# Four small pieces of the opening stage moved to other places in the order of VectorE and ScalarE

## What is computed

```python
xn = _layernorm(x, axis=-1)
x = x + _L0_attn_ref(xn, ...) + _L0_ffn_ref(xn, ...)

# attention: 2 sequences of 1024 tokens, width 256, 16 heads of 16
qkv = xn @ qkv_w.T + qkv_b
scores = q @ k.T / 4 + slopes[h] * (pos_k - pos_q), causal
out = softmax(scores) @ v @ out_w.T + out_b

# experts: 16 of width 128, two for each token
scores = sigmoid(xn @ gate_w)
_, selected = top_k(scores + expert_bias, 2)
routed = sum over the two of weight * (silu(g) * u @ experts_down[e])
shared = silu(xn @ shared_gate_w) * (xn @ shared_up_w) @ shared_down_w
```

## Time and profile before

| | us |
|---|---|
| median of 3 runs | 494.85 (493.16 to 495.5) |
| profiled execution | 498.53 |
| its span in the trace | 496.7 |

### The profile page before, as it was taken

How to read it: one execution, slowest core, us unless ns; L and a number is a source line. 1 busy time by engine, 2 the same in 40 slices (tenths; PEclk the granted TensorE clock), 3 DMA queues, 4 the chain that set the end, 5 groups by cost and what they waited for, 6 DMA issues and landing times.

```text
span 496.7 us, 8349 instructions
## 1 busy us (share of the span) xinstructions
PE 435.9 (88%) x2973; PEld 256.1 (52%) x2973; DVE 324.2 (65%) x602; ACT 248.6 (50%) x567; POOL 181.3 (37%) x200
## 2 busy tenths in 40 slices
PE   3588963489699999998999999999999999999896
PEld 3447842267477667774444344444444444434444
DVE  2869761184457566678875867758687676872366
ACT  1632240130233334334766767667676676766650
POOL 2290677412700000001888887876110100920000
PEclk9799995599999999999999999999999999999999
DMA  8887994168989995434218339173160300002122
GB/s 260 171 355 270 368 326 169 63 214 258 199 181 240 221 247 155 128 96 137 62 46 158 74 73 160 45 130 45 35 114 2 78 18 3 1 2 50 39 69 84
DMA packets 50489, 66.41 MB, mean 134 GB/s; under 512 B 12433, under 2 KB 43285, under 8 KB 48883
## 3 DMA queue, kind: packets, MB, share of 16 engines
q1 hardware_dynamic: 45667, 55.18, 42.1%
q0 software_dynamic: 3680, 10.31, 8.3%
q10 hardware_dynamic: 1104, 0.41, 0.3%
HBM read 39.30 MB, written 27.25 MB: 134 GB/s over the span
## 4 chain that ended last, share of the span: by engine, by line
PE 63%; DVE 15%; DMA 7%; ACT 5%; another core or an unknown queue 5%; issue 4%; SPq 1%; DVEq 0%; ACTq 0%
PE ps L1330 14%; PE ps L1314 11%; PE ps L1302 11%; PE ps L1225 7%; DVE mx L1055 6%; DMA x_in<-sorted_tokens 5%; PE ps L1241 4%; PE ps L1317 3%; PE ps L1303 2%; PE ps L1352 2%; PE ps L1216 2%; DMA x_sb<-x 2%; PE ps L1172 2%; ACT pt L778 2%
## 5 line engine op out<-in xcount | busy, mean ns | idle before, releaser
L778 ACT ACTIVATE pt<-ps 128x512 f32<-128x512 f32 (+3 forms) x384 | 166.7, 492 | 75.3 <-PE ps L1317 48.5
L1055 DVE TENSOR_REDUCE mx<-ps 128x1 f32<-128x384 f32 (+6 forms) x189 | 153.8, 863 | 48.7 <-PE ps L1303 47.3
L1330 PE MATMUL ps<-pt,vg 128*32 128x512 f32 (+3 forms) x768 | 71.9, 492 | 0.0
L619 POOL DMA_INDIRECT yg<-sorted_outputs,slot_i x32 | 32.3, 1011 | 104.4 <-DMA sorted_outputs<-y_out 96.0
L1314 PE MATMUL ps<-qk 111*128 111x512 bf16 (+3 forms) x192 | 54.6, 328 | 3.1 <-ACT pt L778 1.6
L1314 PE MATMUL ps<-qs,ks 111*128 111x512 bf16 (+3 forms) x192 | 55.1, 327 | 0.8
L1225 PE MATMUL ps<-w_gu,hx 128*128 x192 | 52.1, 395 | 3.3 <-issue 1.6
L1302 PE MATMUL ps<-qk 108*128 108x512 bf16 (+3 forms) x192 | 50.2, 328 | 2.7 <-DVE mx L1055 2.2
L1317 PE MATMUL ps<-cbf 128*128 128x128 bf16 x256 | 52.2, 220 | 0.0
L1303 PE MATMUL ps<-cbf 128*128 128x128 bf16 x224 | 46.4, 220 | 0.0
L751 ACT ACTIVATE hx<-ps 128x384 f32<-128x384 f32 (+1 forms) x48 | 22.9, 478 | 40.0 <-PE ps L1216 38.3
(11 more groups left out here) (177 smaller groups left out, 695.1 us busy)
## 6 DMA issues: line engine op xcount, KB each, us to landing
sorted_tokens<-y_out SPq DMA_DIRECT2D x12, 512.0 KB, 5.0
qk_parts<-parts SPq DMA_DIRECT2D x16, 384.0 KB
x_in<-sorted_tokens SPq DMA_DIRECT2D x48, 128.0 KB, 4.9
sorted_outputs<-y_out SPq DMA_DIRECT2D x48, 128.0 KB, 3.0
qk<-qk_parts SPq DMA_DIRECT2D x8, 384.0 KB
w_gu<-e_gu SPq DMA_DIRECT2D x1, 2816.0 KB
x_sb<-x SPq DMA_DIRECT2D x4, 512.0 KB, 9.4
w_dn<-e_dn SPq DMA_DIRECT2D x1, 2048.0 KB
```

Of the source, the lines that this page charges most:

```text
L619: g_.indirect_dma_start(out=yg[:, n % 4, :], out_offset=None, in_=ysd, in_offset=bass.IndirectOffsetOnAxis(ap=slot_i[:, k, t:t + 1], axis= ...
L778: sc.activation(pt[:, s % 4, j, lo:CH], bank(n % 3)[:, lo:CH], ACT.Exp).then_inc(s_exp, 1)
L1055: last = v.reduce_max(dst, src, axis=AX.X)
L1330: ins = te.matmul(ps[32 * j:32 * j + 32, OUT_BANK * CH + lo:(OUT_BANK + 1) * CH], vg[:, par, kb, j, :], pt[:, s % 4, j, lo:CH], start=kb = ...
```

## The change

On ScalarE the high parts of the first two token jobs (numbers 6 and 7) are written between root 2 and root 3, in place of after wsh. On VectorE two weight low parts (jobs 0 and 1) are written after normalise 0 and ahead of statistics 2; and normalise 2, which makes quarter 2's shift, stands ahead of statistics 3 in place of behind it. The other four wl stay where they were. Nothing else differs; the number of instructions on each engine is the same.

```diff
@@ ScalarE
                 if q == 0:
                     for n in range(X0):
                         high(n)
+                if q == 2:
+                    for n in range(X0, X0 + 2):
+                        high(n)
             for q in (2, 3):
                 act.wait_ge(s_shift, q - 1)
...
-            for n in range(X0, G0):
-                high(n)
-            for n in range(G0, NJ):
+            for n in range(X0 + 2, NJ):
                 high(n)
@@ VectorE
-            for q in range(4):
+            for q in range(2):
                 statistics(q)
-                if q in (1, 2):
-                    normalise(q - 1)
-            for q in (2, 3):
-                normalise(q)
-            for n in range(X0):
+            normalise(0)
+            for n in range(2):
+                low(n)
+            statistics(2)
+            normalise(1)
+            normalise(2)
+            statistics(3)
+            normalise(3)
+            for n in range(2, X0):
                 low(n)
```

## The result

| | before | changed |
|---|---|---|
| median, 9 runs each | 494.27 us | 497.73 us |
| ratio of the runs | | 1.0062, 95% interval 1.0037 to 1.0087 |
| profiled execution | 498.53 us | 499.29 us |
| its span | 496.7 us | 497.5 us |
| median, 12 more runs of the changed kernel, 35 of before | 495.34 us | 497.72 us |

A forecast was written before the change was run, and what follows sets the result against it. It took the chain of waits up to the logits to bound this part, with VectorE late until 18.46 us and ScalarE after. Median 494.85 plus 0.92 (order) and 1.1 (clock) gave 496.9 us, range 494.2 to 499.3.

The forecast's parts named there:

- The order on VectorE: Ahead of statistics 3: two wl (0.66 us) and the shift (0.26) delay root 3, first xn and logits by 0.92 us.
- The hole of ScalarE and the early banks: Two xh between root 2 and root 3, and TensorE's earlier transposes of tiles 4 to 7, are hidden: 0 us.
- The clock: Logits: thinner TensorE work ahead leaves some 6 products at 1.2 GHz, 0.19 us more each, 1.1 us.
- Handing on: From slot_i through the 32 scatters to later stages: the delay of some 2 us moves with the path.
- the rival of absorption: Between 78.40 and 97.51 us: a standstill ended by weight loads swallows the delay, 494.85 us; chance 0.06.
- The sum: Whole kernel: 0.92 us of shift and 1.1 us of clock make 2.0 us, median 496.9 us; chance 0.40.
- clock late: Logit stage: 11 products at 1.2 GHz cost 2.1 us, 497.9 us; chance 0.22 together with one more wait.
- Faster by luck further on: Wait of 7.02 us for a tile's load at 160.51 goes if transfers collide less: 489.9 us; chance 0.07.

The follow-up runs named there:

- four wl: The kernel before with four wl in place of two ahead of statistics 2 on VectorE, nothing else: 498.37 us, ratio 1.0041.
- its parts alone: Two kernels, each the kernel before plus one part: two wl ahead of statistics 2, 496.71 us; normalise 2 ahead of statistics 3, 496.00 us.
- VectorE's part: The changed kernel with the two xh back behind wsh on ScalarE, VectorE's new order kept: 497.12 us, ratio 1.0040.
- one-row kernel: The changed kernel, but TensorE's job 8 waits for ScalarE's first xn, so the 24 transposes are one row: 495.14 us, again 496.11 us.
- the kernel with 3.8 us of delay: The kernel before with four unused additions on VectorE right ahead of the choice of experts: 500.32 us, ratio 1.0097.
- shift alone: The kernel before with normalise 2 ahead of statistics 3 and nothing else: 496.00 us, ratio 1.0028.
- two xh alone: The kernel before with two xh between root 2 and root 3 on ScalarE, VectorE as before: 495.45 us, ratio 1.0028.
- small weights in the hole: The kernel before with gwh, wsh and two xh between root 2 and root 3 on ScalarE: 494.09 us, ratio 0.9983.
- o between the g jobs: The kernel with gwh, wsh and two xh in ScalarE's hole, plus the two o jobs between the second and third g job: 494.42 us, ratio 0.9974.

## Why the prediction was right, and where not

**The order on VectorE** (0.92 us): right. 0.89 us at the first xn, 0.91 at the logits; 0.66 and 0.23 us for its parts alone, 1.33 for four wl. Costs by the pitch between neighbours were right, costs by the full duration (1.17) would not have been.

**The hole of ScalarE and the early banks** (0): right. The two xh change nothing on the path, no table load appeared, VectorE's idle time took up what was saved ahead of gwl.

**The clock** (1.1 us): the size was right, by luck as far as the reason goes. The extra time of the logits was 1.5, 1.0 and 1.1 us in the profiles of the change and of VectorE's part of it. My reason was that the split transposes bring the clock back late. But one row of transposes, which by this reason had to cure it, left 9.07 and 8.98 us; and in five of seven profiles the clock was back ahead of the logits and fell again at their start or inside them, a course that I had in no case. Only the other two went as forecast, with a clock that came back inside the logits.

**Handing on**: right against the rival of absorption, by the kernel with 3.8 us of delay. The end of the standstill moves with the scatters. The one-row kernel, late at slot_i by 1.8 us and by its runs hardly slower than before, stays unexplained.

**The sum**: 2.0 us forecast, 1.9 at slot_i in the first profile (1.4 to 1.5 in the second and in VectorE's part; each some 0.4 more against the profiles of shift alone and two xh alone, with their short first addition), and 3.5 and 2.4 us on the medians of two sets of runs. 497.73 lies inside the range, at the place of the case "clock late" (497.9), and by the first set beyond the 0.5% which I had called no difference with a chance of 0.58. (The range's upper end is 499.2 by its own sum, not 499.3.) Of the term behind slot_i, where I had 0, the runs decide nothing: by the medians up to 1.5 us are left over, but 2.0 us, a ratio of 1.0041, lies in the intervals of both sets. How many q/k parts get through before the scatters end is a candidate that I had not seen.

**Faster by luck further on**: a misreading. The wait of 7.02 us at 160.51 isn't in the chain of the changed kernel, and nothing was gained: from the first expert tokens on TensorE to the attention it took 102.2 us before and 102.6 after. A wait in the chain of an iterating stage names one of several things that end nearly together, and isn't a price.

## What to carry to other kernels

An instruction that is put into another place pays with its pitch on the engine that is late there, and gains only where its old place was on the path; look for the idle time behind its old place first. Here the late engine was loaded (two wl, a shift) so that an engine with spare time could be ahead of a wait that was not its own. Where an engine idles for another, move into the hole what the path will need soonest behind it: the small weights, not the parts that stand behind them.

## What was not expected of the hardware

- While the 32 scatters run, and once the transfers had fallen from 377 GB/s (65 to 70 us) to 157 (75 to 80 us), ScalarE and VectorE stood still for long (ScalarE for 19.13 us before, 16.42 changed, 21.20 with the shift alone; VectorE for 16.05 before, in front of an instruction that by the trace had nothing left to wait for), and TensorE issued one product in 1.1 to 1.5 us. ScalarE's last wait of this stretch ended 4.3 to 5.5 us after the last scatter was issued, in all 14 profiles; VectorE could go on earlier (95.39 us before, 2.8 us after the last scatter). No run here shows the cause.
- The clock can fall inside a dense row of products: by 28.29 us in the changed kernel, one microsecond after the logits had begun at full clock. What TensorE did before was 16 transposes until 24.55 and three short jobs.
- The first addition of the choice of experts on VectorE, 128x256, took 0.29 us in most profiles and 0.84, 0.36 and 1.21 us in three (before, two xh alone, small weights in the hole); in these it began before the end of GpSimd's work on aux and ended 0.15 us after it. Running beside that work isn't enough for it: with o between the g jobs it took 0.31 us, 1.6 us ahead of aux's end. No run separates the two.
